# Graph attention over a dense adjacency: the multiply by the adjacency moves to GpSimd, half of the penalties to VectorE, and the sums are taken with the features as weights

## What is computed

```python
xw = x @ W
a_src = xw @ att_src
a_dst = xw @ att_dst
e = leaky_relu(a_src[src] + a_dst[dst], 0.2)
emax = segment_max(e, dst)
ez = exp(e - emax[dst])
coef = ez / segment_sum(ez, dst)[dst]
gat = segment_sum(xw[src] * coef[:, None], dst) + bias
```

## Time and profile before

| | |
|---|---|
| median of the runs | 5028.2 us |
| the profiled execution | 5057.9 us, of which its span is 5056.5 us |
| busy over the span | PE 3077.1 us (61%), DVE 3381.3 (67%), ACT 2077.2 (41%), POOL 1714.8 (34%) |
| the attention over all chunks | from 3967.8 to 4364.2 us of the span |

### The profile page before, as it was taken

How to read it: one execution, slowest core, us unless ns; L and a number is a source line. 1 busy time by engine, 2 the same in 40 slices (tenths; PEclk the granted TensorE clock), 3 DMA queues, 4 the chain that set the end, 5 groups by cost and what they waited for, 6 DMA issues and landing times. The chain is left out here.

```text
span 5056.5 us, 61992 instructions
## 1 busy us (share of the span) xinstructions
PE 3077.1 (61%) x16266; PEld 2263.6 (45%) x16267; DVE 3381.3 (67%) x7048; ACT 2077.2 (41%) x5679; POOL 1714.8 (34%) x1695
## 2 busy tenths in 40 slices
PE   6888888871444444444514444444445588879988
PEld 2444444661333443334413334433344488845444
DVE  8888888534666666667746666666677788553435
ACT  4555555512333333333323333433344578522222
POOL 0000000525666666663056666666630000001210
PEclk7999999985555555555555555555555555589997
DMA  0000000302222222221022222222211200000000
GB/s 19 0 0 0 0 0 0 144 3 64 54 55 53 54 54 55 56 55 44 9 63 55 55 54 55 54 56 55 54 44 56 96 1 1 2 10 4 4 8 7
DMA packets 136541, 183.43 MB, mean 36 GB/s; under 512 B 48763, under 2 KB 110116, under 8 KB 135396
## 3 DMA queue, kind: packets, MB, share of 16 engines
q0 software_dynamic: 50048, 77.77, 6.7%
q1 hardware_dynamic: 85348, 84.60, 6.1%
q10 hardware_dynamic: 896, 18.10, 0.8%
HBM read 158.02 MB, written 22.33 MB: 36 GB/s over the span
## 5 line engine op out<-in xcount | busy, mean ns | idle before, releaser
L1121 POOL DMA_INDIRECT adjacency<-dram_table,sorted_dst x1564 | 1534.7, 981 | 1159.1 <-issue 451.3
L1148 PE MATMUL banks<-adjacency 128*128 x3520 | 779.4, 419 | 535.3 <-ACT adjacency L1180 535.3
L1148 PEld LDWEIGHTS banks<-adjacency 128*128 128x128 f32 x3520 | 759.2, 332 | 578.7 <-issue 578.7
L1218 DVE TENSOR_TENSOR adjacency<-adjacency,banks 128x2048 f32<-128x2048 f32 x110 | 251.8, 2289 | 562.9 <-remote 407.7
L1180 ACT ACTIVATE adjacency<-adjacency 128x2048 f32<-128x2048 f32 x110 | 210.3, 1912 | 876.7 <-DVE adjacency L1218 876.7
L1193 ACT ACTIVATE adjacency<-adjacency 128x128 f32<-128x128 bf16 x1760 | 537.7, 396 | 49.0 <-issue 49.0
L1286 DVE TENSOR_REDUCE adjacency<-adjacency 128x512 f32<-128x2048 f32 x110 | 398.9, 3626 | 166.5 <-ACT adjacency L1193 93.3
L1166 PE MATMUL banks<-ident,largest 128*128 128x128 f32 x440 | 149.4, 392 | 560.2 <-issue 560.2
L1924 PE MATMUL banks<-adjacency,cheb_parts 128*128 128x512 f16 (+1 forms) x2100 | 429.5, 363 | 34.2 <-ACTq L97 31.7
L665 ACT ACTIVATE adjacency<-banks 128x400 f32 x590 | 296.9, 503 | 317.3 <-PE banks L637 311.9
L634 PE MATMUL banks<-cell_hot,src_hot 128*128 128x400 f16 x1180 | 318.7, 352 | 73.9 <-DVE cell_hot L572 73.0
(11 more groups left out here) (496 smaller groups left out, 6164.7 us busy)
## 6 DMA issues: line engine op xcount, KB each, us to landing
adjacency<-dram_src_rows SPq DMA_DIRECT2D x440, 128.0 KB
adjacency<-dram_table,sorted_dst POOLq DMA_INDIRECT x1564
dram_adjacency<-adjacency ACTq DMA_DIRECT2D x1, 17600.0 KB, 46.3
adjacency<-dram_adjacency SPq DMA_DIRECT2D x1, 15387.5 KB, 39.4
dram_table<-adjacency SPq DMA_DIRECT2D x8, 291.0 KB, 5.0
adjacency<-dram_adjacency SPq DMA_DIRECT2D x1, 2212.5 KB, 14.5
dram_nodes<-x_nodes SPq DMA_DIRECT2D x1, 800.0 KB, 4.3
x_nodes<-dram_nodes SPq DMA_DIRECT2D x1, 800.0 KB, 5.8
```

The source lines that it names most:

```text
L1121: pool.indirect_dma_start(ring[:, j % (RG * TG), :], None, dram["table"], bass.IndirectOffsetOnAxis(ap=S.dst_i[:, j:j + 1], axis=0)).then_ ...
L1148: ins = pe.matmul(sums[b % 2][:, s * W1:(s + 1) * W1], reach[:, b % 3, s, t, :], ring[:, bass.ds(at_r[s], TG), :][:, t, 0:W1], start=(t == ...
L1218: dve.tensor_tensor(reach[:, b % 3], reach[:, b % 3], rows[:, :].rearrange("p (s c) -> p s c", c=P).unsqueeze(2).to_broadcast([P, SB, TG, P]),
```

## The change

- VectorE no longer multiplies by the adjacency. GpSimd does, in a queue of its own (`gat_pool`), tile by tile as ScalarE's Exp is done.
- The penalties of odd source blocks (12 of 25 of a chunk) are made by VectorE (`penalize`), those of even blocks stay on ScalarE.
- TensorE takes the features as weights (65 columns) and lets the 512 destinations of `z` pass by: one matmul of each source block in place of four. The sums come out turned (65 partitions by 512). ScalarE copies them to memory (`hold`), TensorE turns them back with a transpose for each 128 destinations (`give_back`) and ScalarE copies these out (`evacuate`), at source blocks 4, 5 and 6 of the next chunk.
- `z` has four buffers (`R` = 4), and the banks are given out anew: two for sums, one for `low` turned, two for the rows, one for what is turned back. Small tiles move to other places in memory.

```diff
-    score = sb("gat_score", [P, 3, NB], F32)
-    far = sb("gat_far", [P, 1], F32)
+    score = sb("gat_score", [P, 2, NB], F32)
+    far = cst.stat[:, 2, 0:1]
...
-    R = 3
+    R = 4
...
+    sums_t, lows_t, rows_in, returned_in = psum[0:2], psum[2], psum[3:5], psum[5]
+    EARLY, BACK, EVEN = 4, 4, -(-NB // 2)
...
+        def hold(c):
+            w = widths[c] * P
+            act.wait_ge(summed.sem, summed.at(c * NB + NB - 1))
+            if c:
+                act.wait_ge(returned.sem, returned.at(c - 1))
+            act.activation(sum_t(c, w), sums_t[c % 2][0:D + 1, 0:w], ACT.Copy).then_inc(held.sem, 1)
+
+        def evacuate(c):
+            act.wait_ge(returned.sem, returned.at(c))
+            act.activation(gat[:, c * CW:c * CW + widths[c], :], returned_in[:, 0:widths[c] * (D + 1)].rearrange("p (n d) -> p n d", d=D + 1),
+                           ACT.Copy).then_inc(evac.sem, 1)
...
+                    if ahead % 2:
+                        continue
...
+        def penalize(c, a):
+            w, i = widths[c] * P, c * NB + a
+            if a == 1 and c:
+                dve.wait_ge(spread.sem, spread.at(c - 1))
+            if i >= PEN:
+                dve.wait_ge(lowest.sem, lowest.at(i - PEN))
+            own_penalty[a] = V.mark(dve.tensor_scalar(pen[:, i % PEN, 0:w], A[:, a, c * CW * P:c * CW * P + w], 0.0, BIG, ALU.is_equal, ALU.mult))
...
-        def weigh(c, a):
-            w, i = widths[c] * P, c * NB + a
-            dve.wait_ge(exps.sem, exps.at(i))
-            dve.tensor_tensor(z[:, i % R, 0:w], z[:, i % R, 0:w], A[:, a, c * CW * P:c * CW * P + w], ALU.mult).then_inc(weighed.sem, 1)
...
+                if a % 2 == 0 and a + 1 < NB:
+                    penalize(c, a + 1)
...
-                behind.append((c, a))
-                if len(behind) > 1:
-                    weigh(*behind.popleft())
...
+    def gat_pool(pool):
+        for c in range(CHUNKS):
+            w = widths[c] * P
+            for a in range(NB):
+                i = c * NB + a
+                pool.wait_ge(exps.sem, exps.at(i))
+                pool.tensor_tensor(z[:, i % R, 0:w], z[:, i % R, 0:w], A[:, a, c * CW * P:c * CW * P + w], ALU.mult).then_inc(weighed.sem, 1)
...
             if a == 0 and c >= 2:
-                pe.wait_ge(evac.sem, evac.at(c - 2))
+                pe.wait_ge(held.sem, held.at(c - 2))
+            w = widths[c] * P
+            pe.matmul(sums_t[c % 2][0:D + 1, 0:w], xw[:, a, :], z[:, i % R, 0:w], start=(a == 0), stop=(a == NB - 1)).then_inc(summed.sem, 1)
+
+        def give_back(c):
+            pe.wait_ge(held.sem, held.at(c))
+            if c:
+                pe.wait_ge(evac.sem, evac.at(c - 1))
+            held_t = sum_t(c, widths[c] * P)
             for j in range(widths[c]):
-                ins = pe.matmul(bank(c, j)[:, 0:D + 1], z[:, i % R, j * P:(j + 1) * P], xw[:, a, :], start=(a == 0), stop=(a == NB - 1))
-            ins.then_inc(summed.sem, 1)
+                ins = pe.transpose(returned_in[:, j * (D + 1):(j + 1) * (D + 1)], held_t[:, j * P:(j + 1) * P], cst.ident[0:D + 1, 0:D + 1])
+            ins.then_inc(returned.sem, 1)
```

More of the change, by code:

```diff
@@ L1589, in gat_attention @@
     near, z = sb("gat_near", [P, 2, CW * P], F32), sb("gat_z", [P, R, CW * P], F32)
-    scaled = sb("gat_scaled", [P, 2, NB], F32)
+    scaled = cst.stat[:, 0:2, :]
+    sum_t = lambda c, w: rows[0:D + 1, c % 2, 0, 0:w]
     penalty, lowest, turned = k.sig("gat_penalty_made"), k.sig("gat_lowest"), k.sig("gat_low_turned")
@@ L1637, in gat_act @@
                 for m in range(2):
-                    ins = act.activation(rows[:, c % 2, m, 0:w], bank(c, m)[:, 0:w], ACT.Copy)
+                    ins = act.activation(rows[:, c % 2, m, 0:w], rows_in[m][:, 0:w], ACT.Copy)
                 ins.then_inc(rows_copied.sem, 1)
@@ L1647, in gat_act @@
                 behind.append((i, w))
+                if c and a == BACK:
+                    hold(c - 1)
+                elif c and a == BACK + 2:
+                    evacuate(c - 1)
             elif what == "last":
                 exponent(*behind.popleft())
[L1650 to L1655, removed]
+        hold(CHUNKS - 1)
+        evacuate(CHUNKS - 1)
     def gat_dve(dve):
@@ L1726, in gat_pe @@
                 pe.wait_ge(lowest.sem, lowest.at(c * NB + NB - 1))
-                if c >= 2:
-                    pe.wait_ge(evac.sem, evac.at(c - 2))
                 for j in range(widths[c]):
-                    ins = pe.transpose(bank(c, CW - 1)[:, j * P:(j + 1) * P], low[:, j * P:(j + 1) * P], cst.ident[:, :])
+                    ins = pe.transpose(lows_t[:, j * P:(j + 1) * P], low[:, j * P:(j + 1) * P], cst.ident[:, :])
                 ins.then_inc(turned.sem, 1)
@@ L1733, in gat_pe @@
                 pe.wait_ge(diags.sem, diags.at(c))
+                if c:
+                    pe.wait_ge(rows_copied.sem, rows_copied.at(c - 1))
                 for m in range(2):
                     for j in range(widths[c]):
-                        ins = pe.matmul(bank(c, m)[:, j * P:(j + 1) * P], cst.ones[:, :], pen[:, m, j * P:(j + 1) * P], start=True, stop=True)
+                        ins = pe.matmul(rows_in[m][:, j * P:(j + 1) * P], cst.ones[:, :], pen[:, m, j * P:(j + 1) * P], start=True, stop=True)
                 ins.then_inc(spread.sem, 1)
@@ L1741, in gat_pe @@
                     sums(*behind.popleft())
+                if c and a == BACK + 1:
+                    give_back(c - 1)
             elif what == "last":
@@ L1744, in gat_pe @@
                     sums(*behind.popleft())
+                give_back(CHUNKS - 1)
                 pe.wait_ge(rows_copied.sem, rows_copied.at(CHUNKS - 1))
@@ L1748, in gat_attention @@
     gat_dve(k.dve)
+    gat_pool(k.pool)
     gat_pe(k.pe)
+    held.close(CHUNKS)
+    returned.close(CHUNKS)
 def gru_gate(k, sb, cst, psum, dram, x, gat):
```

14 lines of the change are left out of this document (7 added, 7 removed).

## The result

The changed kernel takes 5068.7 us (median of 4 runs, 5067.8 to 5069.5), the kernel before 5026.9 us (4 runs, 5024.2 to 5029.0) on the same chip. The ratio is 1.0084, with 95% from 1.0071 to 1.0097: 41.8 us slower, where 45 were forecast.

What follows compares the result with a forecast made beforehand. VectorE was taken to bound the stage, taking turns with GpSimd's multiply: 32 us more for five chunks, 10 for the sixth, 3 for the first low pass, together 45 over 5028.2, so 5073 us; 8-in-10 range 5020 to 5118.

Steps and rivals of the forecast that it cites:

- The sum of a chunk: Everything in a whole attention chunk that must go one at a time: 65.6 us against 59.2, 32 more for five.
- 25 multiplies ... of which 1.02 counts: GpSimd multiplies of a chunk, 1.15 us each, 1.02 counting behind a VectorE instruction: 25.5 us, bounds 22.8 and 28.3.
- Penalties: 12 a chunk on VectorE at 0.35 us: 4.2, bounds 0 and 7.3; sign of taking the ports: ending with a multiply.
- Stalls: VectorE's waits in a chunk: of 7.9 us before, 2.3 remain, bounds 0 and 7.9.
- The exchange with Exp leaves VectorE's queue: VectorE's stalls among near, Relu and Exp go; only the 3.3 us wait for rows stays, partly used by GpSimd.
- Sixth chunk and last: Sixth chunk, penalties and low 128 wide: 41 us becomes 50.8, 10 more; last chunk, bound by ScalarE: 0, between -3 and +3.
- granted clock still near 0.5: Sign of being right: TensorE stays at the lower clock, busy three quarters of a 66 us chunk, waiting on GpSimd.
- multiplies on GpSimd above 1.5 us in the mean: Sign of being right: the attention's GpSimd multiplies, taken as 1.15 us undisturbed, average over 1.5 us.
- The reading of the earlier trace: From other layers: GpSimd and two-input VectorE instructions take turns; beside GpSimd's one-input tensor_scalar VectorE takes 0.29 us, not 1.45.
- No contention: Rival: GpSimd and VectorE overlap, TensorE decides; 4995 us, or 4956 with TensorE at 2.4 GHz; chance 0.13 at either clock.
- Hand-over: Rival: multiplies start late, Exp, multiply and sum stop overlapping the next near; chunk 80 us, 5152 in all; chance 0.13.
- the lock costs about what the multiply frees: Rival: multiply at 0.91, least and half the penalties hidden under it; chunk 58 us, 5029 in all; chance 0.08.

Runs made afterwards that it cites:

- e9: Changed kernel plus a one-input GpSimd operation, z = z * 1.0, ahead of each multiply: 4623.2 us in a single execution, 156 over the kernel before.
- e3: Kernel before with only TensorE's turned sums and four buffers of z; multiply on VectorE, penalties on ScalarE: 4.6 us below the kernel before, ratio 0.9989.
- e4: Changed kernel with a second GpSimd multiply by the adjacency for each source block: 4641.3 us in a single execution, 177 over the kernel before.
- e7: Changed kernel with one of near's row terms and low's running minimum in PSUM banks: 4420.2 us, 46.1 below the kernel before, ratio 0.9897.
- e8: Changed kernel with near and low on PSUM banks and all 25 penalties on ScalarE: 28.5 us below the kernel before, ratio 0.9937.
- e10: Changed kernel with near and low on PSUM banks, all penalties on ScalarE, multiply back on VectorE: 6.5 us below the kernel before, ratio 0.9983.
- e2: Changed kernel with all 25 penalties of a chunk back on ScalarE, multiply still on GpSimd: 14.7 us over the kernel before, ratio 1.0036.

## Why the prediction was right

- **Direction and time.** 5073 forecast, 5068.7 measured. The mechanism, taking turns, held where it was put to the test: doubled it costs 135 us more, with the operands moved to banks it gives 88 us back. What e9 corrects is below.
- **The sum of a chunk**, 65.6 us forecast and 66.95 measured, is right by terms that cancel, and in so far by luck. Instructions are counted as in the prediction, with durations of the five chunks (near 1.034, low 1.080, penalty 0.722 us):

| us | forecast | measured |
|---|---|---|
| near and low by themselves | 33.0 | 33.0 |
| what multiplies add to near, low and least | 25.5 - 2.75 = 22.8 | 25 x 0.288 + 24 x 0.332 + 1.0 = 16.2 |
| penalties | 4.2 | 12 x (0.722 - 0.08) = 7.7 |
| least | 3.3 | 3.3 |
| stalls | 2.3 | 5.7 |
| sum | 65.6 | 65.9, and 1.0 that it doesn't place |

- **The mis-sized term is "25 multiplies ... of which 1.02 counts".** Each was taken to fall on a near or a low in full. The price of one that does was about right, 0.87 us for the 0.91 that are left of 1.02, and so was the 1.15 for a multiply by itself. But beside the 124 multiplies of the five chunks only 89 near and low are lengthened; 19 penalties and five small steps of least make it 113, and the rest hold nothing up. So 0.65 us of each counts in this row, and 0.79 with the penalties' part below, not 0.91.
- **Penalties** were left between 0 and 7.3 us, with 4.2 taken as undisturbed. That is what they cost by themselves (12 x 0.34 = 4.1); with 12 x 0.30 = 3.6 that multiplies hold them up it is 7.7, above the upper end of 7.3, a two-tensor instruction at 0.61 with no hold. The sign named for it is there: the penalty at 4109.40 ends 0.28 us after the multiply.
- **Stalls.** "The exchange with Exp leaves VectorE's queue" was wrong in effect: 5.7 us stay (before, by the same window, 52.5 busy and 6.7 idle, not 51.3 and 7.9). The wait of near for Relu takes 15.7 of the 28.5 us in five chunks, with one of 2.1 to 3.6 us in each; the wait for penalties of ScalarE takes another 10.5.
- **Sixth chunk and last.** +10 forecast, +3.3 measured, by the same over-sized term: up to its last low step it grew from 36.8 to 41.3 us. Near and low average 1.09 and 0.63 us in that time, 1.56 us a block without the overlaps of 0.08, where the forecast had 0.55 + 0.27 + 1.02 = 1.84. The first low pass grew by 1.1 where 3 were forecast.
- **TensorE** was predicted to be hidden, and it is: e3 gains 4.6 us. But the sign "granted clock still near 0.5" was wrong, 0.74. The reason given for it misread: in the window at 0.52 TensorE was busy for 89%, not three quarters. The sign "multiplies on GpSimd above 1.5 us in the mean" was wrong too, 1.30.
- **The reading of the earlier trace rows** was wrong in one point. That GpSimd's tensor_scalar has one input does not by itself leave VectorE's instruction at 1003.29 undisturbed: it starts 1.68 us into it, and e9 shows that one which starts early is held up. A hold "for the whole instruction" is not there either for this operation, only for its first part. Nothing in the sum hung on it. (The high ends of the prediction's terms add up to 77 us as it states them, not 80.)
- **Rivals.** No contention is refuted by e4 and e7, and its 4956 to 4995 (32 to 71 below before) is about where e7 comes out once there is none with near and low: 46 below. Hand-over, at 80 us a chunk, is refuted by the chunk of 66.95 us, of which VectorE idles for 5.7, less than before. That the lock costs about what the multiply frees, 5029 us, is refuted by 5068.7.

## What to carry to other kernels

A count by engines is not enough where work moves from VectorE to GpSimd: first look at where each operand lies. A GpSimd operation beside VectorE instructions that read two tensors from SBUF costs VectorE here 0.65 us of its 1.15, and 0.79 with the penalties that it holds up, more than the 0.60 that leaving the multiply there costs. Put one operand of the VectorE instructions into a PSUM bank, best where TensorE has left it anyway, and the same move gains: 22 us here (e8 for e10) where it cost 19 (e2 for e3), and the change as a whole 46 us (e7) in place of a loss of 42.

## What the runs showed that was not expected

- TensorE's granted clock rose from 0.52 to 0.74 though it was busy for less of the time (201 of 335 us, before 252 of 296). These are means over the five chunks; the clock has two levels, 1.2 and 2.4 GHz, shown as 0.5 and 1. It comes with the new form of the sums, not with the multiply's move: e3, with the multiply on VectorE, has 0.77 and e10 0.78. Where GpSimd fed it more slowly, in e4 and e9, the clock is 0.55 and a matmul of 512 columns takes 1.04 us on average; in e7 they are 0.85 and 0.73. Why the clock rose was not tested. The Trainium skill's page TensorE: Matmul & The Clock Gate, section "What's actually happening", has the chip grant the upper clock by how busy TensorE has been; by busy share alone the trace does not agree, with 0.74 at 60% busy and 0.52 at 85%.
- Size doesn't matter for the turn: 128x4 elements with two inputs waited 1 us for a multiply.
- VectorE's penalties, with one float16 input, are held up by GpSimd: 1.37 us for 0.42.
- A one-input GpSimd operation of 1.92 us holds VectorE up only when VectorE starts early in it (0.50 us in), and then by 0.4 us.
